# New order tables for five queues of a four-layer, one-core kernel

## The chip, the cores and the metric

The kernel runs on one core of a Trainium2 chip. Time is device time of one execution, in microseconds (us). Three runs of the kernel before took 1443.38, 1466.05 and 1468.54 us; the median is 1466.05 us. All data are float32.

## The reference

The input `x` is 8 sequences of 512 tokens with 128 features. Six layers are applied one after the other, each with a residual:

```
x = x + 0.5 * L0_ffn(layernorm(x))     # "ffn1": layernorm, 128->512 ternary weights, gelu, layernorm, 512->128
x = x + L0_attn(layernorm(x))          # "attn": 16-state scan over the 512 tokens, gelu gate, 128->128
x = x + 0.5 * L0_ffn(layernorm(x))     # "ffn2": the weights of ffn1
x = x + 0.5 * L1_ffn(layernorm(x))     # "moef": encode to 256, 64 wide, 8 experts, top 2, back, layernorm
x = x + L1_attn(layernorm(x))          # Mamba: causal convolution, 256 channels x 16 states scanned in chunks of 32
x = x + 0.5 * L1_ffn(layernorm(x))     # "moeb": the weights of moef
```

The eight sequences do not depend on each other. The weights are the same for all.

## The kernel before

**The work.** One sequence (called an image here, number i from 0 to 7) is handled at a time in each stage, as 4 tiles of 128 tokens. Stages of different images overlap. On each engine the work is written as four generators ("threads"), each of which yields between small steps:

- F: for each image ffn1, attn, ffn2 (`f_thread`; lines 500, 718, 950, 1155).
- M: the expert layer, 16 turns (`M_TURNS`, line 34): moef of image i, and three images later moeb of image i - 3 (`moe`, lines 724, 956, 1161).
- P: what comes before the Mamba scan (`before_scan`: mpre, eight steps on PE) and after it (`after_scan`: mout).
- S: the Mamba scan (`s_thread`, lines 549, 846, 1053, 1288): 16 scan steps an image, 128 in all. A step takes two of the 16 states for 128 channels: SP broadcasts B and C rows from a buffer in memory (`bcast`), POOL multiplies them by `du` into `dbu` (L563), ACT makes `dA` by two Exp (L1068), DVE scans over 1024 columns (L858) and multiplies by C (L861), and PE adds the two halves into `yp` with an identity matrix (L1299). After each 8 steps DVE gates the sum (`yg`, L868), which is a step of its own in DVE's S thread: 18 letters S an image there, 16 on the other engines.

An image goes F, moef (M), mpre (P), 16 scan steps (S), mout (P), moeb (M).

**Buffers of the scan.** `dA` has one buffer, in PSUM, so ACT's exponentials of step j wait for the scan of step j - 1 (`hs_r`). `hs` and `dbu` have two, `bcast` has three: DVE's scan j waits for PE's sum j - 2, POOL's j for DVE's scan j - 2.

**The order of the work.** The five queues run in order; a step that waits for another engine holds up all behind it. Which thread's step comes next is written out by hand in the tables of `ORDER` (line 38), one letter a step, read by `side_by_side` (line 70):

```
def side_by_side(order, **threads):
    for t in threads.values():
        next(t)
    for name in order:
        next(threads[name], None)
```

The semaphore waits stand inside the steps and count turns, so that they are the same in any order. The tables have 152 letters for SP (A arrival of x, B the broadcasts, D departure of a result), 240 for POOL, 464 for DVE, 544 for ACT and 616 for PE. Steps differ in size: on DVE the four steps y0 to y3 of an expert turn are two instructions each, the step `stats` is nine; on PE a step is from 2 to 32 matmul records.

Step names used below: on PE an ffn is turn, h01, h2, h3, o0, o1, o2, o3, sq (9 letters F), attn is 4 letters F, an expert turn is turn, enc, s2c, route, he01, he23, he45, he67, y0 to y3, eoT, c2s, dec (15 letters M), mpre is turn, cv0, cv1, res0, res1, mx, dt0, dt1 (8 letters P).

Of the kernel before, what the change touches and what calls it, by code (L numbers as in the profile page):

```python
# [36 lines left out]

ORDER = {
    "SP":
        "AAAABBBBBBABBBBBBBBBBBBBBBBBBABBBBBBBBBDBBBBBBBABBBBBBBBBBBDBBBBBBBABBBBBBBDBBBBBBBBBBBBBBBBBBBBBBDB"  # L40
        "BBBBBBBBBBBBBBBBBBBBBBBBBBBBDBBBBBBBBBBBBBDBBBBBBBDD",
    "Pool":
        "FFFFFFMFFFFFMMMPFFFPFFMMMPSSPSFSFSSSSSFSSSMMSFSMSPSFPSSPMSMSMFSFSSSSFSSSSMMSFSPMSFPSSSPSFFSSMSMMFSSS"
        "SSFSFSMSMPMSPSSPSSFSFSMSMMSSFSSSMMFMSPSSFSPSSSSMPMSMSFSFSSSSFSSSSPMMSFMPSSSSPSSSSSSSSMSMPMSSSPSSSSSS"
        "SSPSSMSMSMSSPSSPSSSSSMSMSMSSSSSSSSSMMMMM",
    "DVE":
        "FFFFFFFFFFFFFFMFMFFFMFMFFMFFMFMMFFFMFMMMPMPFFFFMMFFFFMFMMMPFFFMFMMMMPPPSFSFFSFMMSSFFSSMFMFMFMSPSSSMM"
        "SFMSFMSMFSSSFMMMMMMSPPPMSMPSMMFSMFFSFSMMFSFSFFSMMMFMSSPSSMMSFMSFMSFSMSFSPPPSMMPSMMMMFFFSFSMSMFFMMFMF"
        "SFSPSMMSSMMMMSFFSFSMSMFSMMSMSSPPPMMPSSMMMMFSFFSFMSMMMMFSFSFFSMMFMMMMSSSMMFMFMSMSPFSSMMFMMMMSPSSSSMPP"
        "MSPMMMSFFSFSFMSMSFSFSMFMFSMFMSPSSMMSMFFSMPSMSSSPPSSMMPSSMMSMMSSSSMSMSPMMSMSSPMSMSSSMMSMSMSPSPSSMPSSM"  # L50
        "SMMSMPSSSMMSMPMSMMSSSPSMSMSSMMSMSSSSSMMSSMMSMMSSSMPMMMMMMMMMMMMM",
    "ACT":
        "FFFFFFFFFFFFFFFFFFFMFFMFFFFMMMMFMFFMFFFFMFFFFMMFFFFFFFMPMPMPFMFFMPMFMPMPFFFPMPFFFFMPPPMFPFFMFFFFMSPS"
        "MSMSMFMSFFMFSMSPSPFSPPMFFMSFFFFSMSSPPPSMPMSMSPMMMMMFPPMFFMSFFFFSMSPSPMMSPMSFMFFMMFMSPSMPSFPMSFFMSFFF"
        "FSMSSPPPSPSPMPMFSMFFMFFFMMFMSMSPMMSSFFFMFSPPMSMPPMFSSMFMMFFMFFMFSSMMSSPPSMPSPFPSMFMPPMFFMFFMMFMSMSPS"
        "MSMSFFMFSMFMSMSPMSMMMMFFFMSMFFFFPSMPPPSMPMPSMSPMMMSMPMPPSMSMFSFFSFMFFFSPMSMMSMSMFSMFFMFMSPSPSPPFPSMF"
        "FMSPFPFFSPFMPSPPSSMMSMSMSMMSMPMSSSPSMPMSPSPPSMPPSPSPMMPSMPMSMMSMMSSSSSMSMSSPPSMSPPPMPSMPPSMSPMMMSMPM"
        "PPSSMSMSSSMSSSMSMMSMSMMSMMSSSSMMMMMMMMMMMMMM",
    "PE":
        "FFFFFFFFFFFFFFFFFFFFFFFFMFFMFFFFFMMMMFMFMFMMFMMFFMFFMFFFFFMFFFFFFFFFMPMPFMFMMFPMMPMFMMMFMFPMFFMFFFFF"  # L60
        "MPPPFFFFMFFFFFMSMSMMFMFMSFSSMPMMFSMSMPFPMFSMFFMSFFFFFSSPSPPSMPMSMSMMMMMFMMMMPSMFPMFMFFFFFFSSPSMPMFMF"
        "MMFSSMMPMFSMMSMMSFPMFMSFFMSFFFFFSSPSPPSPSMSFPMFMFFMMFMMFMFMMMMFFMSMSMFSFSFSPFPPMSMFSMFMMFMSMFMFFMMMM"
        "FFMFSMSMSPSPPSFSPFSMPFMSPMFMMFMMFMFMMFMMFSMSMSMFSFPSFMMFSMSMMMMMFMMMMFSMFMFPMFFFFFPSPSPMSMPMSMMMMPMP"
        "MMMMSSMSMSFMFPFFSSFFFFFMSMSMSMMFMFSMSSMPMFMFPMMPSFPMFSMFPFSMPFFFSPFFPSSSSMPMSMSMMMMSMSMMSMMSSPMPSMPM"
        "SPSPSSPPSMPMSMSMMMMSMPMMSMSMSSMSMSMSSPPSPSPMPSMPMSMMMMPMPSMSMMSMSMPMSMSSSSSSMSMMSMMMMSMSMMSMMSSMSMSM"
        "PMMMMMMMMMMMMMMM",
}

# [1268 lines left out]
```

## Time and profile before

| | |
|---|---|
| median of 3 runs | 1466.05 us |
| the profiled execution | 1452.7 us |
| its span, first to last instruction | 1451.0 us |
| TensorE clock granted, mean | 0.816 of full |
| PE busy | 1144.1 us, 79% |
| DVE busy | 1000.1 us, 69% |
| ACT busy | 680.0 us, 47% |
| POOL busy | 601.7 us, 41% |
| first scan step starts, last one's scan ends | 304.0 us, 1373 us |

The busy times are of one execution, and engines overlap. A busy PE is not PE at its full clock: the same four matmul records of `yp` take 1.88 us in one place and 3.71 us in another, at the two levels of the clock.

### The profile page before, as it was taken

The numbers are of one execution on the slowest core, as the hardware profiler recorded it, in microseconds if no ns is written. First come the engines' busy times: TensorE is split into PE (matmuls) and PEld (weight loads), VectorE is DVE, ScalarE is ACT, GpSimd is POOL, SyncE is SP. The second block draws the span as 40 slices with busy tenths as digits, with TensorE's granted clock in tenths as the row PEclk, the third lists the DMA queues.
The fourth block names the chain that finished last, engine by engine and source line by source line (L and its number), as shares of the span: only waits on it lengthen the run. The fifth ranks groups of instructions, "written<-read, shape, count | busy, mean of one in ns | idle before, by whom it ended". The sixth has DMA issues, their size and how long they took to land.

```text
span 1451.0 us, 12541 instructions
## 1 busy us (share of the span) xinstructions
PE 1144.1 (79%) x4326; PEld 666.5 (46%) x4326; DVE 1000.1 (69%) x1607; ACT 680.0 (47%) x1034; POOL 601.7 (41%) x314
## 2 busy tenths in 40 slices
PE   0647889879989897888798798889678776866866
PEld 0425655645547354554445363545335342432425
DVE  2232435377766788877977857899779899698722
ACT  1132445464645545847382555655643624633330
POOL 0012121264543547544553535554655746365210
PEclk9957578777977888979997798979869789797865
DMA  3000000133340335323323323343345445356100
GB/s 92 1 7 8 1 0 8 54 130 116 123 140 29 124 106 162 119 94 116 116 97 123 116 66 118 117 145 117 125 145 174 147 155 175 115 173 210 58 7 8
DMA packets 50840, 142.80 MB, mean 98 GB/s; under 512 B 6741, under 2 KB 17241, under 8 KB 50777
## 3 DMA queue, kind: packets, MB, share of 16 engines
q1 hardware_dynamic: 50776, 142.01, 29.8%
q8 instruction: 34, 0.56, 0.2%
q14 instruction: 30, 0.24, 0.0%
HBM read 139.37 MB, written 2.62 MB: 98 GB/s over the span
## 4 chain that ended last, share of the span: by engine, by line
PE 39%; DVE 34%; ACT 12%; issue 7%; POOL 5%; DMA 2%; SPq 1%; POOLq 0%; DVEq 0%; ACTq 0%
DVE hs L858 14%; PE mp L1200 7%; PE yp L1299 6%; DVE hs L861 5%; PE mp L1191 5%; PE fp L1116 3%; PE fp L1130 3%; ACT he L974 3%; PE fp L1124 2%; POOL dbu L563 2%; ACT L883 2%; DMA bcast<-held 2%; ACT dA L1068 2%; DVE eo L780 2%; DVE f_z L651 2%
## 5 line engine op out<-in xcount | busy, mean ns | idle before, releaser
L563 POOL TENSOR_TENSOR dbu<-du,bcast 128x1024 f32<-128x1024 f32 x128 | 372.3, 2912 | 334.3 <-DVE hs L858 224.3
L1299 PE MATMUL yp<-hs,ident 128*128 128x512 f32 x512 | 300.0, 718 | 75.6 <-DVE hs L861 75.4
L858 DVE TENSOR_TENSOR_SCAN hs<-dA,dbu 128x1024 f32<-128x1024 f32 x128 | 292.5, 2285 | 51.4 <-PE yp L1299 34.7
L1068 ACT ACTIVATE dA<-delta,mA 128x496 f32<-128x496 f32 x256 | 162.9, 669 | 202.7 <-DVE hs L858 201.9
L1299 PEld LDWEIGHTS yp<-hs,ident 128*128 128x128 f32 x512 | 105.7, 223 | 219.5 <-DVE hs L861 112.3
L861 DVE TENSOR_TENSOR hs<-hs,bcast 128x1024 f32<-128x1024 f32 x128 | 175.6, 1372 | 4.4
L1200 PE MATMUL mp<-w_e,he 128*128 128x64 f32 x1024 | 153.8, 323 | 13.7 <-ACT he L974 11.9
L1200 PEld LDWEIGHTS mp<-w_e,he 128*128 128x128 f32 x1024 | 152.3, 238 | 26.5 <-ACT he L974 17.1
L1191 PE MATMUL mp<-cont,w_e 64*128 64x512 f32 x256 | 123.6, 836 | 34.9 <-DVE lg L737 25.1
L974 ACT ACTIVATE he<-mp,vectors 128x512 f32<-128x512 f32 x128 | 82.3, 682 | 90.4 <-PE mp L1191 89.9
L883 ACT ACT_TABLE_LOAD x75 | 96.2, 1283 | 1.3
L1116 PE MATMUL fp<-f_zT,w 128*128 128x512 f32 x128 | 80.1, 756 | 10.1 <-ACT f_zT L903 6.5
L482 POOL TENSOR_TENSOR f_rs<-f_vv,neg_half 128x4 f32<-128x4 f32 x24 | 25.3, 1056 | 149.5 <-DVE f_vv L639 149.2
L778 DVE TENSOR_TENSOR gy<-mp,eo 128x512 f32<-128x512 f32 x64 | 44.1, 688 | 61.4 <-PE mp L1200 60.1
L1191 PEld LDWEIGHTS mp<-cont,w_e 64*128 64x128 f32 x256 | 39.7, 237 | 94.5 <-ACT he L974 51.3
L1124 PE MATMUL fp<-w,hT 128*128 128x129 f32 x512 | 64.8, 283 | 11.0 <-ACT hT L912 11.0
L1124 PEld LDWEIGHTS fp<-w,hT 128*128 128x128 f32 x512 | 61.0, 196 | 25.8 <-ACT hT L912 19.3
L780 DVE TENSOR_REDUCE eo<-gy 128x64 f32<-128x512 f32 x64 | 66.3, 1037 | 2.2
L1130 PEld LDWEIGHTS fp<-w,sq 128*128 128x128 f32 x512 | 65.9, 212 | 0.0
L903 ACT ACTIVATE f_zT<-fp 128x512 f32<-128x512 f32 x24 | 14.2, 592 | 110.1 <-PE fp L1104 110.0
L1130 PE MATMUL fp<-w,sq 128*128 128x1 f32 x512 | 65.6, 262 | 0.0
L678 DVE COPY fs<-fp 128x4 f32<-128x4 f32 x16 | 2.5, 158 | 90.6 <-PE fp L1130 90.6
(204 smaller groups left out, 1653.3 us busy)
## 6 DMA issues: line engine op xcount, KB each, us to landing
bcast<-held SPq DMA_DIRECT2D x128, 1024.0 KB, 5.4
xin<-L_attn_x SPq DMA_DIRECT2D x8, 256.0 KB, 2.9
out<-xo SPq DMA_DIRECT2D x8, 256.0 KB, 3.0
held<-bc SPq DMA_DIRECT2D x8, 64.0 KB, 2.6
he<-conv_wT SPq DMA_DIRECT2D x1, 384.0 KB
w<-w1T SPq DMA_DIRECT2D x1, 256.0 KB
he<-w2T SPq DMA_DIRECT2D x1, 256.0 KB
w_e<-L_ffn_W SPq DMA_DIRECT2D x2, 128.0 KB
```

The source lines that it names most:

```text
L563: pool.tensor_tensor(out=dbu[:, j % 2, :].rearrange("p (r t) -> p r t", r=2), in0=d, in1=b_n, op=ALU.mult).then_inc(dbu_r.sem, 1)
L858: dve.tensor_tensor_scan(out=h, data0=dA[:, :], data1=dbu[:, j % 2, :], initial=0.0, op0=ALU.mult, op1=ALU.add).then_inc(hs_r.sem, 1)
L861: dve.tensor_tensor(out=h, in0=h, in1=bcast[:, j % SLOTS, 1, :], op=ALU.mult).then_inc(hc_r.sem, 1)
L883: act.preload_act_table_set(sets[0])
L974: act.activation(out=he[:, e, :], in_=mps[e % 2], func=ACT.Relu, bias=b_e1[:, e:e + 1]).then_inc(her.sem, 1)
L1068: ins = act.activation(out=dst, in_=src, func=ACT.Exp, scale=mA[:, c, 2 * k + r:2 * k + r + 1])
L1116: pe.matmul(fps[(c + 1) % 2], lhsT=w1[:, c * P:(c + 1) * P], rhs=fzT[:, :], start=True, stop=True).then_inc(h_ps.sem, 1)
L1124: pe.matmul(o[:, q, 0:P + 1], lhsT=hT[:, c, q * P:(q + 1) * P], rhs=w2[:, c, 0:P + 1], start=(c == 0), stop=(c == HC - 1))
L1130: last = pe.matmul(o[:, q, P + 1:P + 2], lhsT=sq[:, c, q * P:(q + 1) * P], rhs=w2[:, c, P + 1:P + 2], start=(c == 0), stop=(c == HC - 1))
L1191: pe.matmul(mps[e % 2], lhsT=w_e1[half, e // 2, :], rhs=cont[half, :], start=True, stop=True).then_inc(he_ps.sem, 1)
L1200: last = pe.matmul(mps[q % 2][:, e * MOE:(e + 1) * MOE], lhsT=he[:, e, q * P:(q + 1) * P], rhs=w_e2[:, e, :], start=True, stop=True)
L1299: last = pe.matmul(yp[:, :], lhsT=ident[:, :], rhs=hs[:, j % 2, r * SEQ:(r + 1) * SEQ], start=(k == 0 and r == 0), stop=(k == PAIRS - 1 an ...
```

## The change

All five strings of `ORDER` are replaced. Each letter occurs as often as before, and no function is touched: every engine issues the same instructions, in another sequence across its threads and the same within each thread.

```diff
--- before.py
+++ after.py
@@ -37,32 +37,32 @@
 
 ORDER = {
     "SP":
...
     "Pool":
...
     "DVE":
-        "FFFFFFFFFFFFFFMFMFFFMFMFFMFFMFMMFFFMFMMMPMPFFFFMMFFFFMFMMMPFFFMFMMMMPPPSFSFFSFMMSSFFSSMFMFMFMSPSSSMM"
-        "SFMSFMSMFSSSFMMMMMMSPPPMSMPSMMFSMFFSFSMMFSFSFFSMMMFMSSPSSMMSFMSFMSFSMSFSPPPSMMPSMMMMFFFSFSMSMFFMMFMF"
-        "SFSPSMMSSMMMMSFFSFSMSMFSMMSMSSPPPMMPSSMMMMFSFFSFMSMMMMFSFSFFSMMFMMMMSSSMMFMFMSMSPFSSMMFMMMMSPSSSSMPP"
-        "MSPMMMSFFSFSFMSMSFSFSMFMFSMFMSPSSMMSMFFSMPSMSSSPPSSMMPSSMMSMMSSSSMSMSPMMSMSSPMSMSSSMMSMSMSPSPSSMPSSM"
-        "SMMSMPSSSMMSMPMSMMSSSPSMSMSSMMSMSSSSSMMSSMMSMMSSSMPMMMMMMMMMMMMM",
+        "FFFFFFFFFFFFFFMFMMMFFFFMMMMFFFFMFMMPPPFFFMFMPSSSSFMFMFSFMMMSMFSFMFMFSFMSSPSPSFFFMFMSSSSSFPFFMFMSMMMF"
+        "MFFFMFMPPMSPSPSFSFFMFMSPSSSFFFMFSMSFSFMSFMMFSMSFSMSMPSMMSFMSPFFSMMFSMMMMSPSMSMSPMSFMFMFSSFSMSMFSFMMM"
+        "MFSFPSMSMFPSMMSSPPMSPFSFFSMFMSSMMPMMSMSMPSSMMSFMSFSFMFMSMMMFMFSFFMFMSSMMSSMPPSPFSFFSMMFSSMMPMMSSMSSM"
+        "PSSMMSMFSFSFMFMSMMMFMFSFFMFMSSPMMSMSPFPSFMMSSSMMMMPSMSSMPSMMSMSSSMMSSMMSMMPSSMSMSMMPMSPSSMMSSSMSMPMM"
+        "SSMPSMSMMSMSSSPMSMSMMSMMSSSMSMSSMMSMSSSMMSMMMMSSMSMPMMMMMMMMMMMM",
     "ACT":
...
     "PE":
-        "FFFFFFFFFFFFFFFFFFFFFFFFMFFMFFFFFMMMMFMFMFMMFMMFFMFFMFFFFFMFFFFFFFFFMPMPFMFMMFPMMPMFMMMFMFPMFFMFFFFF"
-        "MPPPFFFFMFFFFFMSMSMMFMFMSFSSMPMMFSMSMPFPMFSMFFMSFFFFFSSPSPPSMPMSMSMMMMMFMMMMPSMFPMFMFFFFFFSSPSMPMFMF"
-        "MMFSSMMPMFSMMSMMSFPMFMSFFMSFFFFFSSPSPPSPSMSFPMFMFFMMFMMFMFMMMMFFMSMSMFSFSFSPFPPMSMFSMFMMFMSMFMFFMMMM"
-        "FFMFSMSMSPSPPSFSPFSMPFMSPMFMMFMMFMFMMFMMFSMSMSMFSFPSFMMFSMSMMMMMFMMMMFSMFMFPMFFFFFPSPSPMSMPMSMMMMPMP"
-        "MMMMSSMSMSFMFPFFSSFFFFFMSMSMSMMFMFSMSSMPMFMFPMMPSFPMFSMFPFSMPFFFSPFFPSSSSMPMSMSMMMMSMSMMSMMSSPMPSMPM"
-        "SPSPSSPPSMPMSMSMMMMSMPMMSMSMSSMSMSMSSPPSPSPMPSMPMSMMMMPMPSMSMMSMSMPMSMSSSSSSMSMMSMMMMSMSMMSMMSSMSMSM"
+        "FFFFFFFFFFFFFFFFFFFFFFFMFFFMFFMFMMFMFMMMMFMFMFMMFMFFFFPFPFPFPFPFPPPFMFMFMFSFFSFFFMMMMSMSMMSFMFMFSMMS"
+        "MFSFFFFSFFFFFSSPPFPMFSFFSMFFFFSFMSMMMSMFMFMMFMMPPMPFMPMPPFFFFFFSFFFSPSPSPPFPMFSMFFMSFFFFFSSMMPMFMFMP"
+        "FSMSFMMSMPSMMSFMFSFFSFFFFSFPMMSMMMSMMMFMMMMSFMFMSMFSFFSFFFSPSPPMPMSMFPMMFMSFSMMSMMMMFMMSMPPSPSFFSFFP"
+        "FFSFFMFMSMSMMSMPMPMPMPMPMMPSMPMPMSSFFSFFFFFFFSSMMSMSMMMMFMFMMMMSFMMFMSFFSFFSFPFSFFMFMSMPSPMMSMPMPMFS"
+        "MMPMMPSMPMSMSPFSFFSFFSFFFSMMSMSMMMMFMFMMMMSFMMFMSFPFSFFFFFSFFMSMMPMMPMSMSMPMMPMMPSMSMPMSPPSSSMMSMSMM"
+        "MSMMMMSSMMPMMMSSSSMMSMSMMSMPMPMSMPMPMPSMPSMPMPSMSSSSMMSMPMMSMMMSMMSMMSMMSSMSSSSMMSMSMMMSMMMMMMSMMSMS"
         "PMMMMMMMMMMMMMMM",
 }
 
```

## Rows read from the trace of the kernel before

**Rows 1.** The page, part 1: busy time, share of the span and instructions of each engine.
```profile
PE 1144.1 (79%) x4326; PEld 666.5 (46%) x4326; DVE 1000.1 (69%) x1607; ACT 680.0 (47%) x1034; POOL 601.7 (41%) x314
```

**Rows 2.** The page, part 4: the chain of work that ended last, shares by engine.
```profile
PE 39%; DVE 34%; ACT 12%; issue 7%; POOL 5%; DMA 2%; SPq 1%; POOLq 0%; DVEq 0%; ACTq 0%
```

**Rows 3.** Windows: width, busy us of each engine (instructions), clock, DMA share, GB/s.
```profile
52.00:304.00 252.00, 198.03 (x868) 134.50 (x869) 94.07 (x317) 108.06 (x157) 56.65 (x45) 0.73 0.05 16
52.00:127.00 75.00, 41.95 (x183) 27.54 (x184) 23.32 (x85) 21.90 (x30) 13.32 (x12) 0.71 0.01 4
304.00:463.00 159.00, 141.99 (x490) 82.95 (x489) 114.58 (x181) 80.27 (x119) 69.95 (x33) 0.77 0.33 108
463.00:595.00 132.00, 111.26 (x418) 62.05 (x419) 113.34 (x165) 76.29 (x114) 71.92 (x35) 0.87 0.40 132
595.00:757.00 162.00, 141.84 (x584) 80.34 (x582) 130.13 (x208) 97.97 (x147) 81.43 (x41) 0.91 0.33 108
757.00:925.00 168.00, 141.72 (x570) 86.11 (x568) 124.64 (x191) 82.09 (x128) 71.58 (x35) 0.82 0.32 101
925.00:1058.00 133.00, 108.75 (x429) 63.55 (x430) 114.03 (x163) 78.76 (x116) 76.70 (x36) 0.86 0.40 133
1058.00:1170.00 112.00, 89.13 (x268) 41.19 (x268) 97.00 (x102) 53.44 (x87) 61.37 (x25) 0.82 0.45 151
1170.00:1281.00 111.00, 85.79 (x307) 44.98 (x304) 95.31 (x98) 49.12 (x78) 58.89 (x25) 0.88 0.47 153
1281.00:1373.00 92.00, 65.94 (x202) 30.81 (x201) 79.19 (x76) 33.52 (x56) 43.93 (x18) 0.84 0.44 154
1373.00:1451.00 78.00, 50.57 (x166) 31.99 (x165) 21.57 (x58) 16.13 (x30) 6.80 (x6) 0.59 0.02 7
304.00:1373.00 1069.00, 886.42 (x3257) 491.98 (x3257) 868.24 (x1177) 551.46 (x840) 535.77 (x245) 0.84 0.38 126
```

**Rows 4.** Groups, DVE, 304:1373: busy, mean ns | idle before, releasers.
```profile
L858 DVE TENSOR_TENSOR_SCAN hs<-dA,dbu 128x1024 f32<-128x1024 f32 x128 | 292.5, 2285 | 51.4 <-PE yp L1299 34.7 <-ACT dA L1068 12.6 <-POOL dbu L563 2.3
L861 DVE TENSOR_TENSOR hs<-hs,bcast 128x1024 f32<-128x1024 f32 x127 | 174.3, 1373 | 4.3
```

**Rows 5.** Waits, DVE, 304:1373: us in total, times, longest.
```profile
DVE gy L778 <- PE mp L1200: 37.6, 11, 11.3
DVE hs L858 <- PE yp L1299: 34.7, 10, 7.4
DVE yg L868 <- PE yp L1299: 21.7, 9, 4.7
```

**Rows 6.** Timeline, PE: start, us, instruction, count, idle before.
```profile
127.91 0.93 PE L1104 MATMUL mp<-ident,m_z 128*128 128x128 f32 x4
...
178.73 1.06 PE L1104 MATMUL fp<-ident,f_z 128*128 128x128 f32 x4
...
180.48 3.78 PE L1116 MATMUL fp<-f_zT,w 128*128 128x512 f32 x4 [0.69 <-ACT f_zT L903]
...
184.91 2.73 PE L1116 MATMUL fp<-f_zT,w 128*128 128x512 f32 x4
...
189.19 3.74 PE L1124 MATMUL fp<-w,hT 128*128 128x129 f32 x32
...
192.76 3.63 PE L1130 MATMUL fp<-w,sq 128*128 128x1 f32 x32
```

**Rows 7.** Timeline, DVE, 204:308.
```profile
207.57 0.69 DVE L807 TENSOR_TENSOR hx<-m_xp,dd 128x512 f32<-128x512 f32 x1 [3.06 <-POOL dd L522]
...
293.03 1.21 DVE L829 SCALAR_TENSOR_TENSOR delta<-res,cv 128x1024 f32<-128x1024 f32 x1
...
304.02 2.29 DVE L858 TENSOR_TENSOR_SCAN hs<-dA,dbu 128x1024 f32<-128x1024 f32 x1 [0.36 <-ACT dA L1068]
```

More of the change, by code:

```diff
@@ L39 @@
     "SP":
-        "AAAABBBBBBABBBBBBBBBBBBBBBBBBABBBBBBBBBDBBBBBBBABBBBBBBBBBBDBBBBBBBABBBBBBBDBBBBBBBBBBBBBBBBBBBBBBDB"
-        "BBBBBBBBBBBBBBBBBBBBBBBBBBBBDBBBBBBBBBBBBBDBBBBBBBDD",
+        "AAABBBBBBBBABBBBBBBBBABBBBBBBBBBBBABBBBBBBBBBBBBBBBDBABBBBBBBBBBBBBBBBBBDBBABBBBBBBBBBBBBBBBBDBBBBBB"
+        "BBBBBBBBBBDBBBBBBBBBBBBBBBBBBBBBBDBBBBBBBBBBBDBBBBDD",
     "Pool":
-        "FFFFFFMFFFFFMMMPFFFPFFMMMPSSPSFSFSSSSSFSSSMMSFSMSPSFPSSPMSMSMFSFSSSSFSSSSMMSFSPMSFPSSSPSFFSSMSMMFSSS"
-        "SSFSFSMSMPMSPSSPSSFSFSMSMMSSFSSSMMFMSPSSFSPSSSSMPMSMSFSFSSSSFSSSSPMMSFMPSSSSPSSSSSSSSMSMPMSSSPSSSSSS"
@@ L45 @@
-        "SSPSSMSMSMSSPSSPSSSSSMSMSMSSSSSSSSSMMMMM",
+        "FFFFFFMFFFMMPPFFMPSSSSSFSFSSSMFMSSPSSFFMSSSFFPFMPMSSSPSSFSFMSPSSSFFSSSFSSSMPSMSMFSFSSSPSMSMSSFMFSSSS"
+        "PSFSMPMSSMSPSFSFSSSPSMSPMSMSFSSFSSFMSMSMSPSFSFSSSPSSMSPSMSMSFSSFSSFMMSMSSPFSSSSPSMSPMSMSSSSSSSSMSMSM"
+        "PSSSSSSPSSMPSMSMSSSSSSSSSMSMSMSSSSSMMMMM",
     "DVE":
-        "FFFFFFFFFFFFFFMFMFFFMFMFFMFFMFMMFFFMFMMMPMPFFFFMMFFFFMFMMMPFFFMFMMMMPPPSFSFFSFMMSSFFSSMFMFMFMSPSSSMM"
-        "SFMSFMSMFSSSFMMMMMMSPPPMSMPSMMFSMFFSFSMMFSFSFFSMMMFMSSPSSMMSFMSFMSFSMSFSPPPSMMPSMMMMFFFSFSMSMFFMMFMF"
@@ L49 @@
-        "SFSPSMMSSMMMMSFFSFSMSMFSMMSMSSPPPMMPSSMMMMFSFFSFMSMMMMFSFSFFSMMFMMMMSSSMMFMFMSMSPFSSMMFMMMMSPSSSSMPP"
-        "MSPMMMSFFSFSFMSMSFSFSMFMFSMFMSPSSMMSMFFSMPSMSSSPPSSMMPSSMMSMMSSSSMSMSPMMSMSSPMSMSSSMMSMSMSPSPSSMPSSM"
-        "SMMSMPSSSMMSMPMSMMSSSPSMSMSSMMSMSSSSSMMSSMMSMMSSSMPMMMMMMMMMMMMM",
-    "ACT":
[L53 to L58, printed above, removed]
@@ new lines @@
+        "MFFFMFMPPMSPSPSFSFFMFMSPSSSFFFMFSMSFSFMSFMMFSMSFSMSMPSMMSFMSPFFSMMFSMMMMSPSMSMSPMSFMFMFSSFSMSMFSFMMM"
+        "MFSFPSMSMFPSMMSSPPMSPFSFFSMFMSSMMPMMSMSMPSSMMSFMSFSFMFMSMMMFMFSFFMFMSSMMSSMPPSPFSFFSMMFSSMMPMMSSMSSM"
+        "PSSMMSMFSFSFMFMSMMMFMFSFFMFMSSPMMSMSPFPSFMMSSSMMMMPSMSSMPSMMSMSSSMMSSMMSMMPSSMSMSMMPMSPSSMMSSSMSMPMM"
+        "SSMPSMSMMSMSSSPMSMSMMSMMSSSMSMSSMMSMSSSMMSMMMMSSMSMPMMMMMMMMMMMM",
+    "ACT":
+        "FFFFFFFFFFFFFFFFFFMFMFFFFFMFMMMMMFFFMFMMFFFFPFPFFPPPPPPPPPPMFSMFFMSFFSFFMSSMMMMSFFFSFMMSMSFFFSFFSFFP"
+        "SPPFMSMFFSFFSFFMSPPMMMMFMFFFPPMPPMPPPFMSFFFFSFFSPSPSPPPPMFSMPFFPMFFSFFMSSMPMFMFFSFMPSSPSPMSMFSFFFSFM"
+        "SFFMMSMMSMMMMFSFMSMFSFFFSFMSPSPPMPMPSMPMFPSMFFSMFMSMPMMSPSPPPSMFSFFFFFFSMMSPMSMSMMPMPMSPPSPPPPMPMSPP"
+        "FSFFMFFFFSSMMSMSMMMMFMFFSFMMSFMSFFSFFFFSMMSMPSMPPSMMPMSMFPSPPPPMSMPSPPSFFMSFFSFFSMMSMSMMMMFMFFSFMMSM"
+        "FSFFFFFFSMSMMPMSPMPMSMMSPPSPPPMMSPPPPSMSSMMSMSMMMSMMSSMMSSSMSMMSMPSMSMMPMSMPSPPPSPPPMPSMPPSSMSSMMSMM"
+        "SMMMSMSSMSMSSSMSSMMSMSMSMMMMSMMSMMMMMMMMMMMM",
```

## Prediction

> **What bounds the kernel now.** I read the busy times first: PE is busy 79% of the span and DVE 69% [rows 1], so neither alone sets the end. The chain of waits says the same: 39% of it runs over PE, 34% over DVE, 12% over ACT [rows 2]. Then I cut the span at the starts of the eight images' scans [rows 3]. The reader is to see four stretches. Before 304 us nothing is scanned: from 52 us (setup over) PE is 79% busy (198.03 of 252), DVE 37%. From 304 to 925 us PE is 84 to 89% busy: PE and the waits around it bound. From 1058 to 1373 us DVE is 86% busy (271.5 of 315) and PE 76%: the scans bound. The last 78 us is one expert turn alone, at half clock for the most part (0.59). In the scanned stretch the 128 scans and their multiplications take 292.5 + 174.3 us of DVE's 868.2 [rows 3, 4].
>
> The change moves letters only, so I count them. For DVE I count all letters but the 128 scan steps (F, M, P and the two gate steps an image). Old table: 71 before the first scan; then 37, 35, 45, 43, 34, 20, 22 from one image's first scan to the next one's; 13 in image 7; 16 after the last scan. New table: 45; then 49, 33, 40, 42, 40, 30, 22; 19; 16. So 26 letters go from the front to behind the first scan, and the end is as it was. PE has 115 letters before its first scan step before, 74 after. What it is: image 0 is let through; attn, ffn2 of image 2, ffn1 of image 3 and most of moef of image 1 come later.
>
> **The front.** (a) moef of image 0 starts on PE at 127.91 us and its result `hx` is written at 207.57 us [rows 6, 7]. In the old PE table all of ffn2 of image 1 lies between; in the new it follows dec. It costs PE 1.06 + 3.78 + 2.73 + 3.74 + 3.63 = 15 us [rows 6]. PE had hardly any idle time there, so I count all: `hx` at 208 - 15 = 193 us. (b) mpre then takes from 208 to 294 us, since moef of image 1, attn of image 2 and most of three ffns are mixed in. In the new PE table there are 17 letters from dec to dt1 (9 of ffn2, 8 of mpre). A letter of the front costs 198.03/115 = 1.72 us of PE, so 29 us. This stretch will not be dense, since each step needs the one before: the nearest row is the lone expert turn at the end, where PE is busy 50.57 of 78 us, 0.65 [rows 3]. 29/0.65 = 45 us: `delta` at 238 instead of 294. (c) From `delta` to the first scan are 10 us now [rows 7], kept. The first scan starts at 248 us instead of 304: **-56 us**. Bounds: the old front did 71 DVE letters in 252 us, 3.55 us each; 26 fewer would give -92 us. If (a) gives nothing and the stretch is as sparse as 52 to 127 us (PE busy 41.95 of 75, 0.56), 29/0.56 = 52 us and the gain is 34.
>
> TensorE's clock was granted at 0.73 from 52 to 304 us and 0.59 in the sparse tail [rows 3]. If the sparser front fell to 0.59, the 29 us of PE work would take 29 x 0.73/0.59 = 36, and 7 us of the gain would be gone. The Trainium skill, TensorE: Matmul & The Clock Gate, section "The HAM clock gate", says that the throttled level is the default and that activity releases it, a rule that speaks against letting a chain through alone. By it the sum below would be -17 instead of -24; the rows agree with its direction, as the clock is at 0.71 and 0.59 in the two stretches where PE is busy 0.65 or less.
>
> **The 26 letters behind the first scan.** What does a letter cost there? The two fullest stretches (45 and 43 letters) took 162 and 168 us, the two emptiest full ones (20 and 22) 112 and 111 [rows 3]: on the mean 53.5 us for 44 - 21 = 23 letters, 2.33 us each. DVE's own work in one is less, (868.24 - 292.5 - 174.3)/249 = 1.61 us [rows 3, 4]; the rest is waiting and PE. The letters land as +12, -2, -5, -1, +6, +10, 0, +6. The first five add up to 10, in the stretch where PE is full: 10 x 2.33 = 23 us. The other 16 land from 1058 us on, where DVE has 14% and PE 24% idle: I take DVE's own work, 16 x 1.61 = 26 us. Together **+49 us**. Bounds: 26 x 2.33 = 61 us; and nothing, if they vanish in idle time (DVE idle 315 - 271.5 = 43 us late, PE idle 1069 - 886.4 = 183 us in all).
>
> **Hand-overs in the middle.** The old table has 10 places where PE is given 9 or more letters between two scan steps, 128 letters in all; the new has 5, with 70. DVE's scans waited for PE's sum 10 times, 34.7 us [rows 5]. Half of it goes: **-17 us**; bounds 0 and -35. Against this, a step of DVE that needs a step of PE stood two scans behind it in 59 places of 91, one in 27, none in 5; in the new table it is 22, 59 and 20 of 101. That is closer, and at a mean step of 1069/128 = 8.4 us one scan's distance still covers the 2 to 4 us of a PE step. I cost it at nothing; what it costs if that cover is gone is the slower rival.
>
> **POOL, ACT, SP.** DVE's scan waited for `dbu` 2.3 us and for `dA` 12.6 us in 1069 [rows 4], so POOL, the broadcasts behind it and ACT have room. Their tables move with the rest: the broadcasts of an image start earlier, on a queue that moves no more than before. Nothing.
>
> **Sum.** -56 + 49 - 17 = -24 us against the profiled execution's own 1452.7 us: 1428.7, a ratio of 0.983. The median of the runs shown, 1466.05, is 0.9% above that execution; on it the ratio gives **1442 us**.
>
> **Rivals.**
> - **The moved work vanishes.** For it: from 1058 us on both engines have idle time, and the 26 letters need 42 us of DVE's 201 us idle in the scanned stretch. Against it: each letter cost 2.33 us so far, more than its own work. If the 16 late letters cost nothing, the ten early ones 1.61 us each and the hand-overs give 17: -56 + 16 - 17 = -57, that is 1396/1452.7 of 1466, **1409 us**; with the front at -92 it is 1372 us. Chance 0.27.
> - **Slower: DVE stands behind PE.** The place is the 20 steps of DVE (5 before) that follow their PE step with no scan between, most of them y0 to y3 and the route step of moef of images 2, 4, 5, 6 and 7. A wait of `gy` for PE is 37.6/11 = 3.4 us [rows 5]. 15 more of them are +51 us, and a DVE that waits sends its next scan late, so the -17 does not come either: -56 + 49 + 51 = +44, **1510 us**; it is slower than before from 3 of the 15 on (-7 + 3 x 3.4), and by 2% (29 us) from 11 on. Against it: other DVE steps stand in front of some of them, and PE may run ahead. Chance 0.18.
> - **The order does not bind.** The total of idle time stays and only its place moves (the front's 56 us come back as 61 us): **1466 to 1471 us**. For it: the letter price of 2.33 us gives all seven full stretches within 12 us. Chance 0.12.
>
> **How the numbers follow.** The forecast has 0.43, with a range of its own from 1420 to 1470. A measurement of this kernel can tell about 2% from no change, 1437 and 1495 us. Faster by over 2%: the first rival, and a third of the forecast's case, 0.27 + 0.14 = 0.41. Slower: the rival's, 0.18. Within 2%: the rest, 0.41. The range for 8 in 10 goes from 1390, which takes in most of the first rival, to 1490, which leaves most of the slower one out.
>
> **What would show it.** (1) The first scan (L858) starts at 248 us; at over 270 the front step was wrong. (2) `hx` is written first at 193 us. (3) Image 4 takes some 14 us more than 133, image 5 some 16 to 23 us more than 112. (4) DVE's waits for `yp` before the scan fall from 34.7 towards 17 us. (5) The tail from the last scan to the end stays 78 us. (6) If `gy`'s waits for PE pass 60 us in the scanned stretch, the slower rival is at work. The prediction is wrong if the time from first to last scan grows by less than 10 or more than 55 us over 1069.

## The result, and the profile after

| | before | after |
|---|---|---|
| median of 4 runs each | 1461.98 us | 1353.67 us (1350.01 to 1362.26) |
| ratio, 95% interval | | 0.934 [0.9227, 0.9453] |
| profiled execution (span) | 1452.7 us (1451.0) | 1351.33 us (1349.6) |

The new tables are 6.6% faster by the ratio. The ratio leaves out executions over 1.5% above the fastest of the same kernel, as slow ones, so it is not the quotient of the two medians (0.926). The forecast was 1442 us, in a range from 1390 to 1490: the sign was right, and the measured time lies below the whole range.

The page of the changed kernel, part 1 (busy times):
```profile
PE 1086.2 (80%) x4326; PEld 635.8 (47%) x4326; DVE 994.5 (74%) x1607; ACT 681.7 (51%) x1035; POOL 609.9 (45%) x314
```
Part 4 of the same page (the chain of waits, by engine):
```profile
PE 56%; DVE 23%; ACT 12%; issue 5%; POOL 2%; SPq 1%; DMA 0%; POOLq 0%; DVEq 0%; ACTq 0%
```
PE does the same 4326 matmuls in 57.9 us less than in [rows 1], and is idle 43.5 us less (263.4 us of the span instead of 306.9). That is the 101.4 us of the span. The chain of waits has moved on to PE: 56% where [rows 2] had 39%, while DVE fell from 34% to 23%.

The windows of the changed kernel, cut at the same events as [rows 3] (width, busy us of each engine with its instructions, granted clock, DMA share, GB/s):
```profile
52.00:229.00 177.00, 127.67 (x522) 80.75 (x523) 60.66 (x195) 73.28 (x104) 38.88 (x31) 0.70 0.07 22
229.00:405.00 176.00, 153.75 (x636) 91.75 (x634) 131.55 (x226) 104.89 (x149) 77.77 (x41) 0.86 0.30 99
405.00:537.00 132.00, 117.79 (x468) 72.33 (x468) 106.02 (x167) 74.25 (x108) 75.46 (x36) 0.85 0.38 130
537.00:677.00 140.00, 122.08 (x467) 68.00 (x465) 123.68 (x189) 84.22 (x128) 77.06 (x36) 0.88 0.38 125
677.00:811.00 134.00, 122.67 (x539) 71.22 (x540) 119.94 (x196) 86.40 (x131) 77.85 (x38) 0.96 0.38 128
811.00:937.00 126.00, 115.81 (x527) 69.83 (x525) 116.16 (x184) 78.77 (x120) 74.14 (x36) 0.96 0.41 139
937.00:1057.00 120.00, 101.25 (x428) 56.68 (x428) 105.62 (x131) 66.14 (x107) 65.37 (x29) 0.94 0.41 143
1057.00:1169.00 112.00, 82.94 (x249) 38.58 (x250) 99.62 (x110) 54.72 (x90) 68.27 (x29) 0.80 0.45 152
1169.00:1278.00 109.00, 88.29 (x316) 49.92 (x314) 92.76 (x96) 39.63 (x67) 45.58 (x18) 0.83 0.37 129
1278.00:1349.60 71.60, 46.41 (x144) 29.85 (x144) 21.21 (x58) 15.07 (x28) 6.79 (x6) 0.59 0.03 8
229.00:1278.00 1049.00, 904.57 (x3624) 518.31 (x3622) 895.35 (x1292) 589.00 (x896) 561.51 (x260) 0.89 0.38 129
```
The reader is to see three things. The first scan starts at 229 us instead of 304 (75 us gained). From the first scan to the end of the last it is 1049 us instead of 1069, with 26 letters more in it (20 us gained, where the forecast had 32 us lost). The tail is 71.6 us instead of 78. And inside, images 2 to 4 (537 to 937 us) are short for what is in them: image 3 has 42 letters in 134 us, where the old image 3 took 168 us for 43, and the clock there is granted at 0.96 instead of 0.82.

DVE's scans in the changed kernel's scanned stretch (columns as in [rows 4]):
```profile
L858 DVE TENSOR_TENSOR_SCAN hs<-dA,dbu 128x1024 f32<-128x1024 f32 x128 | 292.5, 2285 | 53.1 <-ACT dA L1068 34.1 <-PE yp L1299 13.0 <-POOL dbu L563 5.0
```
DVE's waits in the same stretch of the changed kernel (us in total, times, longest):
```profile
DVE hs L858 <- ACT dA L1068: 34.1, 24, 5.3
DVE gy L778 <- PE mp L1200: 25.0, 13, 6.0
DVE hs L858 <- PE yp L1299: 13.0, 5, 4.3
...
DVE yg L868 <- PE yp L1299: 8.7, 3, 3.7
```
The scans last what they did, 2285 ns. The waits for `yp` before a scan fell from 34.7 to 13.0 us, those of `gy` from 37.6 to 25.0 and those of `yg` from 21.7 to 8.7 [rows 5]; in their place the scan waits longer for `dA` (34.1 us against 12.6 in [rows 4]). So the slower rival's sign (`gy` over 60) did not show.

The front's three marks in DVE's timeline (start, us, instruction, idle before):
```profile
186.36 0.69 DVE L807 TENSOR_TENSOR hx<-m_xp,dd 128x512 f32<-128x512 f32 x1 [3.06 <-POOL dd L522]
...
222.50 1.23 DVE L829 SCALAR_TENSOR_TENSOR delta<-res,cv 128x1024 f32<-128x1024 f32 x1 [1.72 <-ACT cv L1046]
228.67 2.29 DVE L858 TENSOR_TENSOR_SCAN hs<-dA,dbu 128x1024 f32<-128x1024 f32 x1 [4.95 <-POOL dbu L563]
```
The forecast reckoned from the ends: `hx` is written at 187 us (forecast 193), `delta` at 223.7 (forecast 238), and the first scan starts 5 us behind that, where [rows 7] had 10.

### The profile page after: what moved, and what is told of

Read it like the earlier page. It is cut to its first block, busy times and chain, and to the rows that moved or that the text cites. A ratio compares the mean times of both kernels' runs of the same rounds, so it can differ in the third digit from the quotient of the medians.

```text
span 1349.6 us, 12544 instructions
## 1 busy us (share of the span) xinstructions
PE 1086.2 (80%) x4326; PEld 635.8 (47%) x4326; DVE 994.5 (74%) x1607; ACT 681.7 (51%) x1035; POOL 609.9 (45%) x314
## 4 chain that ended last, share of the span: by engine, by line
PE 56%; DVE 23%; ACT 12%; issue 5%; POOL 2%; SPq 1%; DMA 0%; POOLq 0%; DVEq 0%; ACTq 0%
PE yp L1299 12%; PE mp L1200 8%; DVE hs L858 7%; PE mp L1191 6%; PE pp L1241 3%; PE fp L1124 3%; PE fp L1116 3%; PE fp L1130 3%; DVE hs L861 2%; ACT L883 2%; PE mp L1213 2%; PE mp L1169 2%; DVE eo L780 2%; PE mp L1174 2%; SPq L367 1%
## 5 line engine op out<-in xcount | busy, mean ns | idle before, releaser
L563 POOL TENSOR_TENSOR dbu<-du,bcast 128x1024 f32<-128x1024 f32 x128 | 377.2, 2948 | 323.7 <-DVE hs L858 210.7
L1299 PE MATMUL yp<-hs,ident 128*128 128x512 f32 x512 | 290.1, 698 | 65.7 <-DVE hs L861 65.6
L858 DVE TENSOR_TENSOR_SCAN hs<-dA,dbu 128x1024 f32<-128x1024 f32 x128 | 292.5, 2285 | 53.1 <-ACT dA L1068 34.1
L861 DVE TENSOR_TENSOR hs<-hs,bcast 128x1024 f32<-128x1024 f32 x128 | 164.8, 1288 | 4.4
L1200 PEld LDWEIGHTS mp<-w_e,he 128*128 128x128 f32 x1024 | 139.6, 220 | 24.5 <-ACT he L974 13.8
L1200 PE MATMUL mp<-w_e,he 128*128 128x64 f32 x1024 | 139.5, 303 | 6.6 <-ACT he L974 6.6
L1191 PE MATMUL mp<-cont,w_e 64*128 64x512 f32 x256 | 110.7, 723 | 12.4 <-ACT he L974 7.8
L482 POOL TENSOR_TENSOR f_rs<-f_vv,neg_half 128x4 f32<-128x4 f32 x24 | 25.2, 1050 | 127.4 <-DVE f_vv L639 127.1
L1124 PEld LDWEIGHTS fp<-w,hT 128*128 128x128 f32 x512 | 66.4, 207 | 32.5 <-ACT hT L912 25.5
L1124 PE MATMUL fp<-w,hT 128*128 128x129 f32 x512 | 69.5, 294 | 14.5 <-ACT hT L912 14.5
L1191 PEld LDWEIGHTS mp<-cont,w_e 64*128 64x128 f32 x256 | 36.0, 208 | 65.6 <-ACT he L974 39.6
L912 ACT ACTIVATE hT<-fp,vectors 128x512 f32<-128x512 f32 x64 | 42.2, 685 | 27.3 <-PE fp L1116 27.1
L482 POOL TENSOR_TENSOR d_rs<-d_vv,neg_half 128x4 f32<-128x4 f32 x16 | 17.4, 1085 | 85.1 <-DVE d_vv L639 84.0
```

The source lines that it names most:

```text
L563: pool.tensor_tensor(out=dbu[:, j % 2, :].rearrange("p (r t) -> p r t", r=2), in0=d, in1=b_n, op=ALU.mult).then_inc(dbu_r.sem, 1)
L858: dve.tensor_tensor_scan(out=h, data0=dA[:, :], data1=dbu[:, j % 2, :], initial=0.0, op0=ALU.mult, op1=ALU.add).then_inc(hs_r.sem, 1)
L861: dve.tensor_tensor(out=h, in0=h, in1=bcast[:, j % SLOTS, 1, :], op=ALU.mult).then_inc(hc_r.sem, 1)
L1124: pe.matmul(o[:, q, 0:P + 1], lhsT=hT[:, c, q * P:(q + 1) * P], rhs=w2[:, c, 0:P + 1], start=(c == 0), stop=(c == HC - 1))
L1191: pe.matmul(mps[e % 2], lhsT=w_e1[half, e // 2, :], rhs=cont[half, :], start=True, stop=True).then_inc(he_ps.sem, 1)
L1200: last = pe.matmul(mps[q % 2][:, e * MOE:(e + 1) * MOE], lhsT=he[:, e, q * P:(q + 1) * P], rhs=w_e2[:, e, :], start=True, stop=True)
```

## The experiments

The theories after the result. **A, the front**: the gain is the early start of image 0, and the rest costs what its letters cost. **B, the order behind it**: the new order of the scanned stretch does the same letters in less time, because steps meet what they need at the right moment. **C, the long runs of PE**: fewer runs of 9 and more PE letters between scan steps. **D, a faster clock** for whatever reason. In the diffs one line of a table stands for all that differ; "letters" are DVE's without the scan steps, as in the prediction. Ratios are against executions of the kernel before on the same chip. A window is read from one execution of each kernel.

**E1. The old front, the new rest.** The five tables begin as before (DVE's first 72 letters) and end as the new ones (DVE's last 381); in between they are joined. Again 249 letters lie behind the first scan, as before.

```diff
 "DVE" (first row)
-"FFFFFFFFFFFFFFMFMFFFMFMFFMFFMFMMFFFMFMMMPMPFFFFMMFFFFMFMMMPFFFMFMMMMPPPSFSFFSFMMSSFFSSMFMFMFMSPSSSMM"
+"FFFFFFFFFFFFFFMFMFFFMFMFFMFFMFMMFFFMFMMMPMPFFFFMMFFFFMFMMMPFFFMFMMMMPPPSSSSSSSSSSSSSSSSSFPFFMFMSMMMF"
```

> Each table is the old one up to what had ended at 304 us in the trace of before, then the new order of all that is left. The first scan is back at 304 us; the 26 DVE letters that the change moves stand ahead of it again. Theory A (the gain is the early start of image 0, the rest is worth what letters cost): 75 us of the 101 go, so about 1425 us or more. Theory B (the gain lies in how the five tables agree step by step behind the first scan): the new stretch from first scan to end, 1120.6 us, less 26 letters at 1.61 to 2.33 us each, 1060 to 1079 us, on top of 304: 1365 to 1385 us, most of the gain kept.

Measured: 1380.45 us, ratio 0.9653 [0.9501, 0.9805]; profiled span 1371.9 us. Its windows (columns as above):
```profile
52.00:297.00 245.00, 192.44 (x856) 130.75 (x856) 93.52 (x309) 107.68 (x156) 55.48 (x45) 0.73 0.05 17
297.00:833.00 536.00, 462.25 (x1770) 255.04 (x1771) 448.42 (x660) 301.42 (x451) 283.85 (x135) 0.88 0.39 129
833.00:1301.00 468.00, 387.11 (x1520) 212.55 (x1519) 415.11 (x519) 239.28 (x382) 253.50 (x112) 0.89 0.43 140
297.00:1301.00 1004.00, 849.36 (x3288) 467.59 (x3288) 863.53 (x1178) 540.70 (x832) 537.34 (x246) 0.88 0.41 134
```
And the halves of the scanned stretch of the kernel before:
```profile
304.00:925.00 621.00, 536.80 (x2058) 311.44 (x2057) 482.70 (x743) 336.62 (x505) 294.88 (x142) 0.84 0.34 111
925.00:1373.00 448.00, 349.62 (x1199) 180.53 (x1200) 385.54 (x435) 214.84 (x336) 240.89 (x104) 0.85 0.44 147
```
With the old front the scanned stretch takes 1004 us, where the kernel before takes 1069 for the same 249 letters: **65 us come from the order alone**. By PE's rows: busy 849.4 us instead of 886.4 [rows 3], which is 37 us, and idle 155 instead of 183, which is 28 us. The 37 us are what the granted clock would give: 886.4 x 0.84/0.88 is 846. Against the changed kernel (1049 us, 275 letters) the 26 letters cost 45 us, 1.7 us each. E1's front is 68 us longer than that of the changed kernel (297 us to its first scan against 229), so the new front with its letters is worth 22 us of span, net.

How firm is this split? The profiled executions of E1 and of the kernel before are 79 us apart, E1's being the fastest of its four; the ratio of 0.9653 makes it some 50 us, with an interval from 28 to 72. The old tables gave nearly the same windows in two more executions (622 us in E3 for images 0 to 3, 449 in E4 for images 4 to 7, where before has 621 and 448), but E2's images 1 to 7, on the old tables too, took 925 us instead of 910. So the order behind the front carries about half of the gain by the ratios, and three quarters by the profiled executions; the 65 us are uncertain by some 15 us or more.

E1 holds the total of letters, not where they stand. From its first image to its last it has 23, 33, 40, 42, 40, 30, 22 and 19 letters, where the kernel before has 37, 35, 45, 43, 34, 20, 22 and 13. Three of its images:
```profile
297.00:429.00 132.00, 100.89 (x300) 46.93 (x300) 95.19 (x112) 56.59 (x86) 55.04 (x27) 0.81 0.40 130
699.00:833.00 134.00, 122.27 (x538) 71.07 (x539) 119.93 (x195) 86.59 (x131) 77.46 (x38) 0.96 0.39 128
833.00:962.00 129.00, 117.12 (x529) 69.72 (x529) 116.35 (x186) 79.45 (x122) 74.32 (x36) 0.95 0.42 135
```
Image 0 takes 27 us less for 14 letters fewer, no more than the old price of a letter would give (33 us). Image 3 takes 34 us less for one letter fewer, and image 4 takes 4 us less with 6 letters more. There the gain cannot be put down to the number of letters.

DVE's waits in E1's scanned stretch:
```profile
DVE hs L858 <- ACT dA L1068: 31.2, 19, 9.1
DVE gy L778 <- PE mp L1200: 22.2, 9, 6.4
DVE yg L868 <- PE yp L1299: 15.4, 6, 3.8
...
DVE hs L858 <- PE yp L1299: 5.6, 6, 2.7
```
The waits for `yp` before the scan are 5.6 us, where before had 34.7. So the gain behind the front comes with no change to the front, as B has it.

**E2 and E4. The new tables up to the start of image 1 (E2) or of image 4 (E4), then the old ones.** The letters that the new front leaves out then have to come back in one place, before the image at the seam (on PE in one run of 52 letters in E2 and of 40 in E4).

```diff
 "DVE" (first row)
-"FFFFFFFFFFFFFFMFMFFFMFMFFMFFMFMMFFFMFMMMPMPFFFFMMFFFFMFMMMPFFFMFMMMMPPPSFSFFSFMMSSFFSSMFMFMFMSPSSSMM"
+"FFFFFFFFFFFFFFMFMMMFFFFMMMMFFFFMFMMPPPFFFMFMPSSSSFMFMFSFMMMSMFSFMFMFSFMSSPSPSFFFMFMSSSSSFPFFMFMSMMMF"
```
(of E4; E2 changes back at the end of image 0)

> The new order up to what had ended at 405 us (first scan of image 1) in the trace of the changed kernel, then the old order of what is left; 14 DVE letters more than the old table has are still open there and come next. Theory A: image 0 starts at 229 us and image 1 at 405 plus the open letters, 14 x 2.33 = 33, against 463 in the kernel before: 438 + 989.7 (the old rest) = 1428 us, 25 less than before. Theory B: the rest runs as in the kernel before and the early scans only leave other work behind: 1440 to 1465 us.

> The new order up to 811 us (first scan of image 4 in the changed kernel), then the old order of what is left, 22 DVE letters more than the old table has there. Letters that cost what they cost (theory A with images 2 and 3 faster): 811 + 526 + 22 x 2.33 = 1388 us. Theory B in its strict form (the first 811 us are fast because they leave 22 letters open, and the old order pays them back): the 64 letters between the first scans of images 3 and 4 come without scans beside them, at the 3.55 us a letter of the front, 811 + 526 + 78 = 1415 us, or up to 1450 us.

Measured: E2 1467.09 us, ratio 1.025 [1.009, 1.0409], above both theories' times; E4 1434.3 us, ratio 0.9999 [0.9943, 1.0054]. The window of E2's image 0:
```profile
232.00:475.00 243.00, 205.35 (x835) 128.12 (x833) 153.21 (x292) 124.95 (x180) 88.85 (x48) 0.80 0.21 72
```
The windows of E4's image 3 and of its images 4 to 7:
```profile
676.00:912.00 236.00, 200.95 (x824) 124.62 (x824) 151.57 (x280) 111.93 (x174) 86.66 (x46) 0.81 0.23 75
912.00:1361.00 449.00, 352.90 (x1212) 181.46 (x1213) 386.35 (x436) 217.10 (x339) 239.47 (x103) 0.85 0.44 145
```
Both have the early first scan (232 us), and both lose it at the seam. E2's image 0 holds 63 letters where the changed kernel's holds 49: 243 us against 176, so the 14 cost 4.8 us each. E4's image 3 holds 64 where the changed kernel's holds 42, and takes 236 us against 134: 4.6 us each, with DVE busy 151.6 of 236. A letter that finds no scan to stand beside costs at least what it does in the front (3.55 us by the prediction). So the front's 75 us are worth something only if the letters that leave it find scans to stand between; A alone gives nothing in these two. E4's images 4 to 7, which run on the old tables, take 449 us, as in the kernel before (448): the gain of B is not carried over into them.

**E3. The old tables up to the start of image 4, then the new order.**

```diff
 "DVE" (third row)
-"...SPFSSMMFMMMMSPSSSSMPP"
+"...SPSSSPPSP"
```

> The old order up to 925 us (first scan of image 4), then the new order of what is left, which has 22 DVE letters fewer left than the new table alone. If what is left costs what it costs in the changed kernel (538.6 us from its image 4 on) less 22 letters at 1.61 to 2.33 us: 925 + 487 to 503, 1412 to 1428 us, so that the new order of the late images is worth 25 to 40 us. If the new order is good only on top of its own past: about 1450 us. The gain of images 2 and 3 is left out in both.

Measured: 1449.69 us, ratio 1.0072 [0.9995, 1.0148]. Its windows, images 0 to 3 and 4 to 7:
```profile
306.00:928.00 622.00, 533.07 (x2064) 308.53 (x2063) 486.48 (x745) 337.59 (x505) 295.14 (x143) 0.85 0.34 111
928.00:1379.00 451.00, 349.47 (x1220) 181.08 (x1220) 377.98 (x435) 211.84 (x334) 240.95 (x104) 0.86 0.44 146
```
Images 4 to 7 take 451 us in the new order and 448 in the old, with the same 89 letters. **The late part of the new order is worth nothing**, for a table that comes to it as the old one does; the seam leaves image 4 with 18 letters, where the old order has 34. E1 agrees for the most part: it does its images 0 to 3, with 138 letters, in 536 us, where the kernel before has 621 us for 160. At 1.7 us for each of the 22 letters between, 48 of those 85 us are the order. Images 4 to 7 of E1 hold 22 letters more than before's and take 468 us against 448; that leaves 17 us to the order there, which E3 does not bear out.

**E5. Only the long runs of PE split.** In the old PE table ten scan steps move forward by 5 to 11 letters into the runs of 9 and more; the other engines keep the old tables.

```diff
 "PE" (second row)
-"...PPSMPMSMSMMMMMFMMMMPSMFPMFMFFFFFFSSPSMPMFMF"
+"...PPSMPMSMSMMMMMSFMMMMPMFPMFMSFFFFFFSPSMPMFSM"
```

> The kernel before; in PE's table alone the scan letter behind each of the 10 runs of 9 or more letters is moved to the middle of its run, so that PE sums a scan step up to 11 letters earlier. The prediction's step on hand-overs: DVE's scans waited 34.7 us for such sums, half or more of it goes, 1420 to 1435 us. Theory B (one table changed alone loses its agreement with the others: PE now stands before a sum that is not ready and holds back steps which ACT and DVE wait for): no gain or slower, 1450 to 1480 us.

Measured: 1453.7 us, ratio 1.009 [1.001, 1.0171]. No gain: C falls, for the old tables. In its scanned stretch the scans' waits for `yp` fell from 34.7 to 27.2 us, and their waits for `dA` rose from 12.6 to 31.1: one wait went and another came. E7 below speaks against C too: its PE table has ten runs of 9 or more letters, 113 in all, nearly as many as the old one, and it keeps 5% of gain.

**E6, E11 and E10. One engine's table a single letter out of step.** In E6 every scan step of the new PE table stands one letter later (120 of 128 could be moved), in E11 one letter earlier (117). E10 does to the kernel before what E6 does to the changed one (121). All else stays.

```diff
 "PE" (first row of E6, then of E11)
-"...FMFMFMFSFFSFFFMMMMSMSMMSFMFMFSMMS"
+"...FMFMFMFFSFFSFFMMMMMSMSMFSMFMFMSMM"
...
-"...FMFMFMFSFFSFFFMMMMSMSMMSFMFMFSMMS"
+"...FMFMFMSFFSFFFFMMMSMSMMSMFMFMSFMSM"
 "PE" (second row of E10)
-"MPPPFFFFMFFFFFMSMSMMFMFMSFSSMPMMFSMSMPFPMFSM..."
+"MPPPFFFFMFFFFFMMSMSMFMFMFSMSSPMMFMSMSPFPMFMS..."
```

> The changed kernel; in PE's table alone 120 of the 128 scan letters change places with the letter behind them, so that each sum comes one step later (the other 8 would lock up). Nothing else is changed. If the order binds only coarsely (letters per image, as my prediction counted them), a PE step of some 1.7 us among 8 us a scan step is lost in slack: 1350 to 1365 us. Theory B: each step waits for one more step of PE, in a chain that runs over all engines: 120 times up to 1 us, 1400 to 1470 us.

> The changed kernel with 117 of the 128 scan letters of PE's table one letter earlier, the mirror of e6. If e6 was slow only because sums came late, earlier sums are harmless: 1340 to 1370 us. Theory B: PE then stands before a sum whose scan has not run and holds up the step that ACT or DVE waits for: 1420 to 1540 us, like e6 or worse.

> What e6 does to the changed kernel, done to the kernel before: in PE's table 121 of the 128 scan letters one letter later. In e6 it cost some 94 us. If the old tables agreed with each other as well as the new (theory B has the gain from somewhere else then, such as fewer letters in flight), it costs as much: 1540 us or more. If the old order is slow because its tables agree badly, much of that waiting is there already and the shift costs little: 1440 to 1490 us.

Measured: E6 1448.17 us, ratio 1.0044 [0.9999, 1.0088], which is 1.0044/0.934 = 1.075 of the changed kernel (1.070 by the medians). E11 1526.16 us, ratio 1.0561 [1.0352, 1.0769], 1.13 of the changed kernel. E10 1582.87 us, ratio 1.0959 [1.0784, 1.1134]. Part 1 of E6's page:
```profile
PE 1110.3 (77%) x4326; PEld 648.4 (45%) x4326; DVE 987.7 (68%) x1607; ACT 682.5 (47%) x1035; POOL 614.7 (43%) x314
```
Part 1 of E11's page:
```profile
PE 1146.3 (75%) x4326; PEld 662.3 (43%) x4326; DVE 987.6 (65%) x1607; ACT 681.7 (45%) x1035; POOL 612.4 (40%) x314
```
E6's span is 95 us longer than the changed kernel's: PE is busy 24 us more and idle 71 us more. In E11 it is 177 us: 60 busy, 117 idle. The waits over the whole run say where (us in total, times, longest). DVE's in E6:
```profile
DVE hs L858 <- PE yp L1299: 59.8, 22, 6.0
...
DVE yg L868 <- PE yp L1299: 47.5, 12, 9.4
```
PE's largest in E11:
```profile
PE yp L1299 <- DVE hs L861: 175.5, 63, 10.1
```
The same wait in the changed kernel:
```profile
PE yp L1299 <- DVE hs L861: 65.6, 23, 7.6
```
DVE's largest in E10:
```profile
DVE hs L858 <- PE yp L1299: 142.2, 39, 8.8
```
A scan step of PE that comes late makes DVE wait for `yp`: 59.8 us in E6, where the changed kernel waits 13.0, and 142.2 in E10, where the kernel before waits 34.7. One that comes early makes PE wait for `hs`, 175.5 us instead of 65.6. **The place of PE's scan steps, to the letter, is worth more than the whole change.** That is what B needs, and it does not prove B. E10 speaks against it in part: the expectation had it that tables which agree badly would not mind the shift, and that 1540 us or more would mean that the old tables agree with each other as well as the new. They lose 120 us of span, more than the new ones' 95. So both orders are set to the letter; that the new one fits better is not shown by the shifts.

**E7, E8 and E9. Three further sets of tables, with all five engines' letters reordered step by step.** E7's letters are ordered anew by moves of up to 12 places. E8 and E9 are meant to keep DVE's instructions with two SBUF operands away from POOL's (the last section tells why). Each differs from the changed kernel in 203 to 216 of DVE's 464 letters and 288 to 298 of PE's 616.

```diff
 "DVE" (first row; -: changed kernel, +: E7, E8, E9)
-"FFFFFFFFFFFFFFMFMMMFFFFMMMMFFFFMFMMPPPFFFMFMPSSSSFMFMFSFMMMSMFSFMFMFSFMSSPSPSFFFMFMSSSSSFPFFMFMSMMMF"
+"FFFFFFFFFFFFFFMFMMFMFFFMMMMFFFFMMFMPPPFFMFMPFSSMSSSMFSFFMFMSMFMFSFFSFMMSMSPSFPFFMFMSSPMSFFFSFMSMMMMF"
+"FFFFFFFFFFFFFMFMFMFMFFFMMMMFFFFMMFMPPPFFFMFMPSMSSMSSFFFMMFSMMFFSFMFSFMSMSPPSFFFSFMMSSSSMFMSFFFMPMMMF"
+"FFFFFFFFFFFFFFFMMMFFFFMMMMMFFFFMFMMPPPFFFMMFPSSSSMFFFMFSMSMMMFSFMFFSMFSSMPPSSFFFMFMSSSMSFFFPFMMSMSMM"
```

> The changed kernel with all five tables ordered anew by single letters moved by up to 12 places, with durations of the steps from the trace of the changed kernel; 45 DVE letters before the first scan as in the changed kernel, and per image at most 5 letters more or fewer. Prediction's counting: letters are where they were, so 1350 us. Theory B: what is left to gain is the waiting between engines in the scanned stretch. Images 3 and 4 of the changed kernel have DVE 91% busy; if the whole stretch with its 895 us of DVE work came to that, it would take 984 us instead of 1049: 1286 us. I expect half to all of it, 1285 to 1320 us.

> The changed kernel with its five tables ordered anew by single letters, as in e7, but what is added up now lets POOL's multiplications and those DVE steps that read two operands from SBUF exclude each other, as the traces show it (107 DVE instructions of the changed kernel last 144 us longer than their like, and 70 of them end 0.1 us after a dbu of POOL ended). Letters per image stay within 3 of the changed kernel's. Theory B with this term (e7 fell short because its order pushed DVE steps into POOL's: 172 us lost that way, 28 more): clearly faster than 1354, 1260 to 1320 us, with under 120 us lost to it. Theory B without it: this order has no advantage over the changed kernel's, 1350 to 1370 us. Letter counting: 1350 us.

> A second order found in the same way from another start of the search; its letters between scans differ from those of e8. If what it is fitted to is real, both are faster than the changed kernel; this one, which came out 1% longer when added up, 1270 to 1335 us. If one of them was luck: one near 1350 us or above.

Measured: E7 1373.29 us, ratio 0.9502 [0.9451, 0.9553]; E8 1355.25, 0.933 [0.9289, 0.9371]; E9 1374.6, 0.9476 [0.942, 0.9533]. None reached the time that theory B expected of it, and none beats the changed kernel; E8 equals it, which its expectation had as the sign that the new term gives no advantage, and E9 is above it. Part 1 of E8's page:
```profile
PE 1090.1 (81%) x4326; PEld 635.3 (47%) x4326; DVE 945.2 (70%) x1607; ACT 675.7 (50%) x1031; POOL 580.4 (43%) x314
```
E8 took 49 us of busy time off DVE (994.5 to 945.2) and the time did not move, since PE's busy time stayed at 1090 us and its idle time at 258. That fits a kernel bound by how PE and the scans meet, no longer by DVE's own work; but E8's order differs as a whole, so it does not prove it. Three sets that agree with the new one in little more than half of their places all land from 1355 to 1375 us, so the gain is not one lucky order. But all three keep the new tables' letters per image within 4, and E7 and E8 were made from them.

## Why the prediction was wrong

The four terms, as the prediction put them and as the runs measured them (spans; E1 divides the order from the letters):

| step | forecast | measured |
|---|---|---|
| front | -56 (-34 to -92) | -75 |
| 26 letters behind the first scan | +49 (0 to +61) | +45 (1004 to 1049) |
| hand-overs in the middle | -17 (0 to -35) | **-65** (1069 to 1004) |
| tail | 0 | -6 |
| sum | -24 | -101 |

The middle two rows are divided as E1 divides them, which is not quite as the forecast did: in E1 all 26 letters are missing from image 0, and its other letters stand as in the new tables. At the prediction's own prices E1's placing of letters is worth 11.5 us of the 65 (16 letters fewer up to image 4 at 2.33, 16 more behind it at 1.61), and 53 are left. That is still three times the forecast, and past its bound.

**The step that failed is the hand-overs.** It took the gain of the new order to be what DVE waited for `yp`, halved, with 35 us as its bound. Three things were wrong in it.
- *The quantity.* Long runs of PE stood for the fit of the tables. E5 splits the runs and gains nothing; E6 moves each scan step by one letter, which leaves the five runs as they are, and loses 95 us. So a count of runs does not give the time. That the distance between where PE stands and where DVE stands, step by step, does is the reading that E6 and E11 suggest; no run measures it for the old order against the new.
- *The bound.* A wait on DVE is only one side. The kernel before had 183 us of PE idle in the scanned stretch [rows 3]; the prediction wrote that number down, as room for letters, and did not ask what of it a better order could take away. It took 28 us in E1. DVE's idle time fell with it, from 201 to 140 us, though its waits for `yp` before a scan fell by only 29.
- *What follows from it.* The same matmuls took 37 us less of PE's busy time in E1's scanned stretch, at a granted clock of 0.88 instead of 0.84. The prediction knew the clock only as a threat in the front. The Trainium skill, "TensorE: Matmul & The Clock Gate", section "The HAM clock gate", says that activity releases the higher level. The traces agree at the ends: the two stretches of the changed kernel with PE 0.92 busy (677 to 937 us) have 0.96, and its tail, 0.65 busy, has 0.59. They do not agree throughout, since 304 to 463 us of the kernel before is 0.89 busy at 0.77. Whether the closed gaps raise the clock or the clock closes gaps no run here separates, so theory D is neither shown nor ruled out.

**The front** was right in mechanism and too small, -75 for -56. `hx` came 6 us earlier than forecast. From there to `delta` it took 37 us where 45 were reckoned. The window of that stretch in the changed kernel:
```profile
187.00:222.50 35.50, 28.25 (x107) 14.56 (x105) 11.99 (x44) 18.56 (x26) 12.88 (x9) 0.84 0.19 52
```
PE's work in it is 28.25 us, the 29 of the forecast; but PE is busy 0.80 of the time, not 0.65. A likely reason, not tested, is that the letters of ffn2 stand between those of mpre there, while the lone expert turn has nothing beside it. The last 5 us gained are those between `delta` and the first scan. The threat from the clock did not come true here: it is granted at 0.84 in this stretch. In the whole front it is 0.70, where before had 0.73. The prediction's own bound of 3.55 us for a letter would have given 92.

**The letters** came out near, 45 us for 49, with luck in it: at the prediction's prices the 26 letters by which the changed kernel's image 0 exceeds E1's would cost 61 us, and the rest would give 11.5 back. The price of 2.33 us is no constant. It is 1.7 us for those 26, which stand between scans, 0.9 us for the 22 that E1 has more than the kernel before in images 4 to 7 (468 us against 448), and 4.6 to 4.8 us where letters are heaped before one image (E4, E2). The price law of the old table, 62.6 us an image and 2.33 us a letter, gives the new images 0, 1, 6 and 7 within 8 us, and images 2 to 5 took 16, 26, 30 and 12 us less than it says: a law read from one order does not hold for the next.

**The rivals.** The slower one lived on 20 steps of DVE that follow their PE step closely; `gy` waited 25.0 us for PE, less than before. The one that came nearest is the first, in sign and size, with the wrong reason: the moved letters did not vanish, they cost 45 us, and the order paid for them. "The order does not bind" was given 0.12 and is refuted by E1, E6, E10 and E11 alike. Of the marks, (1), (2) and (4) went the way of the forecast and beyond; (3) failed, as image 4 took 126 us instead of 147 and image 5 120 instead of 128 to 135, and (5) did not hold by 6 us. The scanned stretch shrank by 20 us where less than 10 us of growth was to prove the prediction wrong.

**What stays open.** Why the new order is faster. By the windows the gain lies in images 2 to 4 above all, but which pairs of steps carry it, and in which engine's table, is not known: no set was tried in which one engine's new table stands beside the others' old ones. A rival is untested: that it is enough to move letters from the crowded images to the late ones, in whatever fine order. Against it speaks image 3, which is 34 us shorter with one letter less; for it, that E7 to E9 keep the new counts and three quarters or more of the gain. Clock and gaps are not separated. And the seams of E2 to E4 add an error to what they say of one part alone.
